# Opening stage of an int8-style cross-attention kernel: key batches ahead of the last four query tiles, query load in two parts, group 0 values quantised on GpSimd, key bias as three 16-bit parts

## The chip, the cores and the metric

One core of a Trainium2 chip. The metric is the device time of one execution in microseconds; lower is better. Names of engines: TensorE (PE, its weight loads PEld), VectorE (DVE), ScalarE (ACT), GpSimd (POOL), and SyncE (SP), whose queue issues every DMA of this kernel. Each engine works through its own instructions in the order in which they are written; semaphores tie the engines together.

## What is computed

1600 tokens of 512 channels attend with 16 heads of 32 channels to 5776 context rows, and a gated feed-forward block follows. Queries, keys, values and the softmax output are rounded to 8-bit grids:

```python
q = (x @ Wq + bq).reshape(1, B * N, H, hd)            # x: layer norm of the tokens
kv = (cond @ Wkv + bkv).reshape(1, -1, 2, H, hd)
q = _fq_sym(q * scale, axis=-1)                        # step: max|q| / 127 of a token and head
k = _fq_sym(k, axis=-1)
v = _fq_sym(v, axis=2)                                 # step over all 5776 rows
attn = _fq_unsigned(softmax(einsum('bhqd,bhkd->bhqk', q, k)), axis=-1)
out = einsum('bhqk,bhkd->bhqd', attn, v) @ Wp + bp
x = x + out;  x = x + ffn(layernorm(x))
```

## The kernel before

**Stages.** (1) The opening: the key and value projections of head group 0 (four of the sixteen heads) and the queries of all heads. (2) The loop over 200 tiles of (head, 128 tokens), i = 0 to 199, in which the projections of groups 1 to 3 are interleaved. (3) The output projection and the feed-forward block. The change is in the opening, in the first tiles of the loop, and in one matmul of every projection.

**Key units and batches.** The context is cut into 46 units of 128 rows (the last has 16). `unit(g, u)` on PE computes the keys of a unit into half of a PSUM bank (L539, four fp32 matmuls, each of which the profile shows as two), adds the key bias with a matmul of its own (L546, `e0` whose row 0 is one, times `bk_b`), and computes the values transposed (L541). Units alternate between the banks PO and PK, so a unit waits (`s_kve`) until ACT has moved out the unit two before it: `unit_out` copies keys to KB (L711) and values to VF (L713). Twelve batches of up to four units make group 0. For a batch b, DVE's `batch` takes maxima of keys and values (L877, L881) and a reciprocal (L884), POOL's `k_scale` scales KB (L1090), ACT's `k_round` rounds through int8 (L719, L724), POOL's `k_parts` (L1102, L1105, L1111) and ACT's `k_high` (L736) split the result in three bf16 parts in KS, and SP's `store_k` writes them to DRAM (L318). KS is one buffer, so parts of a batch wait (`s_kd`) for the store of the batch before it.

**Query tiles.** For each of 13 tiles of 128 tokens DVE's `layernorm(t)` takes statistics (L901 to L903), ACT takes a square root (L742, `x_sqrt`), DVE normalises (L905, L908); PE transposes (L560), ACT copies to XNT (L748), PE multiplies by WQ (L569); DVE quantises (L925 to L936) into QS, and SP stores it (L405). The order in the opening is written out by hand: PE does batch 0 and then, for t = 0 to 12, the query of tile t, the transpose of tile t + 1, and batch t + 1. DVE does layer norm t + 2, batch t, query t. ACT does the root of tile t + 2, XNT of t + 1, the four `unit_out` of batch t + 1, `k_high` of t - 1, `k_round` of t.

**The end of the opening.** SP's queue then holds, in this order: weights and first units of group 1, three quarters of head 0's keys transposed into KT (L374), the last query and key stores, the last quarter of KT, all of QT (L365), and three transposes that turn the values VI (L427). Before these DVE has quantised the values of group 0 from VF to VI (L949, L950, six instructions). Behind them stand the context loads CT (L303) of the loop's first units.

**The loop.** For tile i PE computes scores in four chunks (L592), DVE moves them out with a running minimum (L966), ACT takes exponentials to 8 bits (L790), SP transposes them (L463), POOL spreads them into PT (L1154), and four tiles later PE multiplies by the values (L611), which ACT moves to AO (L776). Between the chunks PE does quarter slices of the units of the step.

Of the kernel before, what the change touches and what calls it, by code (L numbers as in the profile page):

```python
# [39 lines left out]
P = 128  # L40
# [42 lines left out]
MAGIC = 12582912.0  # L83
LN255 = float(np.log(255.0))
EPS = 1e-5
F16_UNIT = float(2.0 ** 24)

# [45 lines left out]
def build(nc, x, ctxt, ctxl, Wq, bq, Wkv, bkv, Wp, bp, w13T, w2T, norm_w, eye, Qd, Kd, Vd, Od, out):  # L133
    ctx = ExitStack()
    with ctx:
# [8 lines left out]
        e0 = sb("e0", [P, P], F32)  # L144
        bk_b = sb("bk_b", [P, 2, GC], F32)
# [38 lines left out]
        KT = [None] * 3  # L184
        for r in (1, 0, 2):
            KT[r] = tmp(f"KT{r}", [KEYS], BF16)
        QT = ring("QT", 3, [NT * P], BF16)

        with ExitStack() as early:
            WQ = tmp("WQ", [NK, C], F32, early)  # L190
            XT = ring("XT", 2, [C], F32, early)
            XN = ring("XN", 2, [C], F32, early)
            XNT = ring("XNT", 2, [NK, P], F32, early)
            QF = tmp("QF", [H, HD], F32, early)
            QG = tmp("QG", [H, HD], F32, early)
            QS = ring("QS", 2, [H, P], BF16, early)
            BQ = tmp("BQ", [C], F32, early)
# [7 lines left out]
        AO = ring("AO", 2, [NT, 2 * HD], F32)  # L205
# [7 lines left out]
        with ExitStack() as unsplit:  # L213
# [26 lines left out]
        names = """cst s_x0 s_x1 s_w s_sd s_xn s_tp s_tpe s_q s_qe s_qs s_qd0 s_qd1 s_wg s_wg1 s_bk0 s_bk1 s_bv s_ku s_kve  # L240
                   s_kr s_kn s_ki s_kc s_k6 s_k8 s_kh s_kd s_kl s_kp s_vd0 s_vd1 s_vr s_vt s_vg s_vi s_wp s_qk s_ev s_mx s_exp s_pad s_pvp s_pv s_pve s_rz
# [55 lines left out]
        def _(sp):  # L297
# [25 lines left out]
            def load_wg(g):  # L323
                if g:
                    sp.wait_ge(M["s_ku"], g * NU)
                sp.dma_start(bk_b[:, g % 2, :], bkv[g * GC:(g + 1) * GC].partition_broadcast(P)).then_inc(M[f"s_bk{g % 2}"], 16)
                sp.dma_start(WG[:, :, 0, :], wkv_v[:, :, g * GC:(g + 1) * GC]).then_inc(M["s_wg"], 16)
                sp.dma_start(WG[:, :, 1, :], wkv_v[:, :, C + g * GC:C + (g + 1) * GC]).then_inc(M["s_wg1"], 16)
# [30 lines left out]
            def load_head(h, piece):  # L359

                if piece == 0:
# [3 lines left out]
                    sp.dma_start_transpose(QT[h % 3].rearrange("p (a n) -> p a n", a=1), Qd[:, h, :]).then_inc(s_qt[h % 3], 16)  # L365
# [10 lines left out]

            load_x(0)
            load_wg(0)
            for u in range(RING):
                load_unit(0, u)  # L380
            sp.dma_start(ident[:, :], eye).then_inc(M["s_w"], 16)
# [7 lines left out]
            for t in range(NT):  # L389
                if 2 <= t:  # L390
                    store_k(0, t - 2)
                if t + 3 < NT:
                    load_x(t + 3)
                while nxt < min(NU, NB * t + 10):
                    load_unit(0, nxt)
                    nxt += 1
                if t == NT - 1:

                    load_wg(1)
                    for u in UNITS[-1]:  # L400
                        load_unit(*u)
                    for piece in range(1, NC_):
                        load_head(0, piece)
                sp.wait_ge(M["s_qs"], t + 1)
                sp.dma_start(Qd[t * P:(t + 1) * P], QS[t % 2]).then_inc(M[f"s_qd{t % 2}"], 16)  # L405
            for b in range(NT - 2, NBT):
                store_k(0, b)
            load_head(0, NC_)

# [11 lines left out]
            sp.wait_ge(M["s_qd0"], 16 * (-(-NT // 2)))  # L421
            sp.wait_ge(M["s_qd1"], 16 * (NT // 2))
            load_head(0, 0)
            for n, lo in enumerate(VT_LO):
# [3 lines left out]
                                       VI[1][:, lo:hi, :].rearrange("p u c -> p (u c)")).then_inc(M["s_vi"], 16)  # L428
            for s in range(3):
# [92 lines left out]
        def _(pe):  # L522
            def unit(g, u, slices=range(NK)):
# [12 lines left out]
                for c in slices:  # L536
# [6 lines left out]
                    if c == 1:  # L543
                        if u == 0:
                            pe.wait_ge(M[f"s_bk{g % 2}"], 16 * (g // 2 + 1))
                        pe.matmul(bank[0:n, 0:GC], e0[:, 0:n], bk_b[:, g % 2, :], start=False, stop=True)  # L546
# [4 lines left out]
            for u in BATCH[0]:  # L551
                unit(0, u)
            pe.wait_ge(M["s_w"], 16 * 3)

# [8 lines left out]
            x_transpose(0)  # L563
            for t in range(NT):
                pe.wait_ge(M["s_tpe"], t + 1)
                if t:
# [5 lines left out]
                if t + 1 < NT:  # L572
                    x_transpose(t + 1)
                for u in (BATCH[t + 1] if t + 1 < NBT else []):
                    unit(0, u)
            for u in UNITS[-1]:
                unit(*u)

            def scores(i, c):
# [3 lines left out]
                if c == 0:  # L583
                    for h, *_r in segs:
                        pe.wait_ge(s_kt[h % 3], 16 * NC_ * (h // 3 + 1))
                        pe.wait_ge(s_qt[h % 3], 16 * (h // 3 + 1))
# [110 lines left out]
        def _(act):  # L697
# [53 lines left out]
            for u in BATCH[0]:  # L751
                unit_out(0, u)
            x_sqrt(1)
            x_transposed(0)
            for t in range(NT):
# [4 lines left out]
                for u in (BATCH[t + 1] if t + 1 < NBT else []):  # L760
                    unit_out(0, u)
# [7 lines left out]
            def values_out(i):  # L769
                p, segs = tile_of(i)  # L770
                j = i % PAIRT
                act.wait_ge(M["s_pv"], i + 1)
                if j == 0 and p >= 2:
# [76 lines left out]
        def _(v):  # L850
# [3 lines left out]
            v.memset(e0[:, :], 0.0).then_inc(chain.sem, 1)  # L854
            chain.n += 1
            chain.sync()
# [399 lines left out]
```

## Time and profile before

| | |
|---|---|
| runs shown | 2012.63, 2016.89, 2017.28 us; median 2016.89 |
| profiled execution | 2016.73 us, of it the span 2014.9 us |
| opening, until the loop's first unit has its context | 194.7 us of the span |
| PE, DVE, ACT, POOL busy over the span | 86%, 83%, 67%, 74% |
| granted PE clock, mean | 0.85 of full speed |

The profiled execution is 0.16 us from the median, so sums made against it stand for the median too. The timeline lists instructions in order of time; what stands in brackets is how long the engine was idle before it and what released it. Busy shares over the whole span mix the opening, where PE sets the pace, with the loop, where DVE does.

### The profile page before, as it was taken

How to read it: one execution, taken by the hardware profiler on the slowest of the kernel's cores; microseconds unless marked ns; L12 is line 12 of the kernel's file. 1: busy time of each engine (PE TensorE's matmuls, PEld its weight loads, DVE VectorE, ACT ScalarE, POOL GpSimd, SP SyncE). 2: the span in 40 equal slices, each digit the busy share in tenths (PEclk: the TensorE clock that was granted, in tenths of full speed). 3: DMA queues.
4: the chain of work that ended last, by engine and by line, in shares of the span. 5: the costliest groups of instructions: out<-in, count | busy, mean ns of one | idle time of the engine just before them, and what ended most of it. 6: DMA issues, size and time to landing. Idle time of an engine off the chain costs nothing.

```text
span 2014.9 us, 40535 instructions
## 1 busy us (share of the span) xinstructions
PE 1729.9 (86%) x16230; PEld 1168.7 (58%) x16230; DVE 1682.1 (83%) x2664; ACT 1357.6 (67%) x1293; POOL 1499.8 (74%) x1182
## 2 busy tenths in 40 slices
PE   7995888898788888887888888788988897699996
PEld 6884666665556666565666664344444444467774
DVE  5775999999889999997899999899999997464552
ACT  2441888888678788886888888677777776322221
POOL 1342698988898888989889889988987977255453
PEclk9997999998989999898999996566556555799998
DMA  4656899999989999999799997978877766513311
GB/s 160 204 180 176 159 199 199 185 199 189 211 173 202 178 184 187 172 213 195 166 202 193 179 194 166 186 133 166 155 140 139 149 116 116 170 43 75 77 44 43
DMA packets 862442, 323.11 MB, mean 160 GB/s; under 512 B 789104, under 2 KB 817712, under 8 KB 862256
## 3 DMA queue, kind: packets, MB, share of 16 engines
q1 hardware_dynamic: 862256, 320.53, 76.1%
q8 instruction: 129, 2.11, 0.4%
q14 instruction: 57, 0.47, 0.1%
HBM read 80.87 MB, written 46.20 MB: 63 GB/s over the span
## 4 chain that ended last, share of the span: by engine, by line
DVE 35%; PE 21%; issue 16%; POOL 15%; DMA 5%; ACT 4%; SPq 3%; POOLq 0%; DVEq 0%; ACTq 0%
DVE S L966 32%; POOL PT L1154 9%; PE PS L653 6%; PE PS L592 6%; PE PK L687 3%; DMA PP<-Pr 3%; PE PK L670 2%; PE PK L539 2%; ACT Pr L790 1%; PE PO L611 1%; SPq L463 1%; POOL VQ L1123 1%; POOL KD L1102 1%; POOL VB L1126 1%; POOL KE L1105 1%
## 5 line engine op out<-in xcount | busy, mean ns | idle before, releaser
L966 DVE TENSOR_SCALAR_CACHE_REDUCE S<-PS,SQN 128x1536 f32<-128x1536 f32 (+1 forms) x768 | 1285.7, 1714 | 90.2 <-PE PS L592 73.9
L790 ACT ACTIVATE Pr<-S,MS 128x5888 uint8<-128x5888 f32 x200 | 1041.4, 5207 | 249.7 <-DVE MJ L981 174.6
L1154 POOL CAST PT<-PP 128x1536 uint16<-128x1536 uint8 (+1 forms) x800 | 1094.5, 1413 | 93.3 <-DMA PP<-Pr 92.0
L592 PE MATMUL PS<-KT,QT 96*128 96x512 bf16 (+1 forms) x2496 | 785.7, 446 | 118.1 <-DVE S L966 106.2
L611 PEld LDWEIGHTS PO<-VI,PT 128*128 128x128 f16 x9200 | 364.6, 102 | 360.9 <-issue 185.7
L611 PE MATMUL PO<-VI,PT 128*128 128x32 bf16 x9200 | 376.4, 183 | 96.1 <-ACT AO L776 61.7
L592 PEld LDWEIGHTS PS<-KT,QT 96*128 96x128 bf16 (+1 forms) x2496 | 215.2, 108 | 316.3 <-issue 183.2
L539 PE MATMUL PK<-WG,CT 128*128 128x128 f32 (+1 forms) x1272 | 226.8, 309 | 34.0 <-DMA CT<-ctxt 20.1
L541 PE MATMUL PK<-CT,WG 128*128 128x128 f32 (+1 forms) x1272 | 210.6, 293 | 0.0
L539 PEld LDWEIGHTS PK<-WG,CT 128*128 128x128 f32 (+1 forms) x1272 | 178.0, 204 | 37.7 <-DMA CT<-ctxt 21.6
L541 PEld LDWEIGHTS PK<-CT,WG 128*128 128x128 f32 x1272 | 166.5, 193 | 1.3 <-issue 0.3
L1090 POOL TENSOR_TENSOR KB<-KB,kam 128x512 f32<-128x512 f32 (+1 forms) x48 | 48.6, 1012 | 147.4 <-DVE kam L884 147.4
L653 PE MATMUL PS<-W,XIF 128*128 128x512 f32 (+3 forms) x624 | 144.1, 387 | 3.6 <-POOL XIF L1209 3.6
L653 PEld LDWEIGHTS PS<-W,XIF 128*128 128x128 f32 (+1 forms) x624 | 114.2, 187 | 30.7 <-issue 5.4
L711 ACT ACTIVATE KB<-PK 128x128 f32<-128x128 f32 (+1 forms) x159 | 42.7, 269 | 91.8 <-PE PK L541 78.9
L1102 POOL TENSOR_TENSOR KD<-KE,kam 128x512 f32<-128x512 f32 (+1 forms) x48 | 50.6, 1055 | 70.7 <-ACT KE L724 70.7
L687 PE MATMUL PK<-W,IQF 128*128 128x512 f32 (+1 forms) x286 | 72.0, 409 | 14.5 <-POOL IQF L1203 11.5
L842 ACT ACTIVATE TG<-G 128x1408 f32<-128x1408 f32 (+1 forms) x13 | 17.9, 1377 | 79.9 <-DVE G L1043 79.9
L687 PEld LDWEIGHTS PK<-W,IQF 128*128 128x128 f32 (+1 forms) x286 | 54.5, 192 | 29.3 <-POOL IQF L1203 12.4
L1043 DVE SCALAR_TENSOR_TENSOR G<-PS,sc,TG 128x1408 f32<-128x1408 f32 (+1 forms) x13 | 21.9, 1682 | 52.3 <-PE PS L653 52.3
L546 PE MATMUL PK<-bk_b,e 128*128 128x128 f32 (+1 forms) x318 | 64.2, 285 | 0.0
L966 DVE DVE_READ_ACCUMULATOR S<-PS,SQN 128x1 f32 x768 | 63.8, 83 | 0.0
(125 smaller groups left out, 1417.5 us busy)
## 6 DMA issues: line engine op xcount, KB each, us to landing
CT<-ctxt SPq DMA_DIRECT2D x180, 256.0 KB, 3.3
k_rows<-KS SPq DMA_DIRECT2D x44, 512.0 KB, 3.9
v_rows<-VS SPq DMA_DIRECT2D x33, 256.0 KB, 3.8
VQ<-v_rows SPq DMA_DIRECT2D x33, 256.0 KB, 3.8
q_rows<-QS SPq DMA_DIRECT2D x13, 512.0 KB, 2.6
W13F<-w13T SPq DMA_DIRECT2D x16, 352.0 KB, 4.4
attn_out<-AO SPq DMA_DIRECT2D x8, 416.0 KB, 5.2
PP<-Pr SPq DMA_TRANSPOSE x200, 6.0
```

Of the source, the lines that this page charges most:

```text
L539: pe.matmul(bank[0:n, 0:GC], CT[k % RING][:, d, 0:n], WG[:, d, 0, :], start=(d == 0), stop=False)
L541: last = pe.matmul(bank[:, GC:GC + n], WG[:, d, 1, :], CT[k % RING][:, d, 0:n], start=(d == 0), stop=(d == NK - 1))
L546: pe.matmul(bank[0:n, 0:GC], e0[:, 0:n], bk_b[:, g % 2, :], start=False, stop=True)
L592: last = pe.matmul(PS[n % 2][p0:p0 + r, f:f + w], QT[h % 3][0:PARTS * HD, q0:q0 + r], KT[h % 3][0:PARTS * HD, c * CHUNK + f:c * CHUNK + f ...
L611: last = pe.matmul(PO[:, 0:w], PT[i % 2][:, u, :].bitcast(F16), VI[g % 2][:, u, h * HD:h * HD + w], start=(u == 0), stop=(u == NU - 1))
L653: last = pe.matmul(PS[half][0:n, f:f + w], XIF[:, c, 0:n], W13[:, c, a, half * FF + f:half * FF + f + w], start=(c == 0 and a == 0), stop= ...
L687: last = pe.matmul(PK[0:n, :], IQF[:, k, 0:n], W2[:, k, a, :], start=(k == 0 and a == 0), stop=(k == NF - 1 and a == WPARTS - 1))
L790: act.activation(Pr[i % 2].rearrange("p t q b -> p t b q"), S[i % 2].rearrange("p (t b q) -> p t b q", b=2, q=P), ACT.Exp, bias=MS[:, i % ...
L966: v.tensor_scalar(S[i % 2][:, c * CHUNK:c * CHUNK + CW[c]], PS[n % 2][:, 0:CW[c]], neg_step, None, ALU.mult, ALU.min, accum_out=MN[:, i % ...
L1090: gp.tensor_tensor(KA, KA, kam[:, kb % 2, 1, 0:m].unsqueeze(2).to_broadcast([P, m, HD]), ALU.mult).then_inc(M["s_kn"], 1)
L1102: gp.tensor_tensor(v3(KD), v3(KE), kam[:, kb % 2, 0, 0:m].unsqueeze(2).to_broadcast([P, m, HD]), ALU.mult).then_inc(M["s_k6"], 1)
L1154: gp.tensor_copy(PT[i % 2][:, 2 * t0:2 * t1, :].rearrange("p (t b) q -> p t b q", b=2), PP[i % 2][:, t0:t1, :].bitcast(U8).rearrange("p t ...
```

## The change

- Each of the first nine key batches (0 to 8) is followed by its query tile, as before; batches 9, 10 and 11 then follow without one, and query tiles 9 to 12 come after batch 11 (`Q_AFTER`). SP issues the transposes of KT as the batches are stored, and QT of head 0 in two parts: tiles 0 to 8 (`s_q0`) ahead of the last key stores, tiles 9 to 12 (L374 of the new file) behind the turning of the values.
- The six instructions that quantise group 0's values move from DVE to the end of POOL's opening (L1230, L1231 of the new file), behind the parts of batch 11. The scale is taken by DVE right after batch 11.
- The key bias of all groups is split by DVE, once, in three bf16 parts held in rows 0 to 2 of BK3 (seven instructions, L909 to L915); the bias matmul of every unit of every group is a bf16 one with `ones`.
- The scaling of the query by 1/sqrt(32) (L927) goes into other constants; QG is dropped.
- ACT takes the root of tile b + 2 **ahead of** `unit_out` of batch b.
- The clearing of QS comes after the start signal, that of AO moves to the start of the loop and to tile 4. DVE no longer waits for the query stores before it pads S. KT, QT and AO of the third or second buffer, and the early tiles, trade places in SBUF.

```diff
-            for t in range(NT):
-                if t + 2 < NT:
-                    x_sqrt(t + 2)
-                if t + 1 < NT:
-                    x_transposed(t + 1)
-                for u in (BATCH[t + 1] if t + 1 < NBT else []):
-                    unit_out(0, u)
-                if 1 <= t <= NBT:
-                    k_high(0, t - 1)
-                if t < NBT:
-                    k_round(0, t)
+            for b in range(NBT):
+                for t in Q_AFTER[b][:1]:
+                    if t + 2 < NT:
+                        x_sqrt(t + 2)
+                for u in BATCH[b]:
+                    unit_out(0, u)
+                if b == 0:
+                    x_transposed(0)
+                if b >= 2:
+                    k_high(0, b - 2)
+                if b:
+                    k_round(0, b - 1)
+                for t in Q_AFTER[b][:1]:
+                    x_transposed(t + 1)
...
-                        pe.matmul(bank[0:n, 0:GC], e0[:, 0:n], bk_b[:, g % 2, :], start=False, stop=True)
+                        pe.matmul(bank[0:n, 0:GC], ones[:, 0:n], BK3[:, g * GC:(g + 1) * GC], start=False, stop=True)
...
+            gp.wait_ge(M["s_vr"], 1)
+            for n, lo in enumerate(VT_LO):
+                hi = VT_LO[n + 1] if n + 1 < len(VT_LO) else NU
+                q = VF[:, lo * P:hi * P]
+                link(gp.tensor_scalar(q, q, VS3[:, 0, 2:3], MAGIC, ALU.mult, ALU.add))
+                gp.tensor_scalar(VI[1][:, lo:hi, :].rearrange("p u c -> p (u c)"), q, 1.0, -MAGIC,
+                                 ALU.mult, ALU.add).then_inc(M["s_vt"], 1)
```

ScalarE around the first units of batch 1, before (sd is the root of a tile, XNT the copy of a transpose, KB and VF the two halves of `unit_out`):

```order
L742 ACTIVATE sd<-mv 128x1 [waits s_sd]
L748 ACTIVATE XNT<-PS 128x512 [waits s_tp]
L742 ACTIVATE sd<-mv 128x1 [waits s_sd]
L748 ACTIVATE XNT<-PS 128x512 [waits s_tp]
L711 ACTIVATE KB<-PK 128x4x32 [waits s_ku]
L713 ACTIVATE VF<-PK,BV 128x128
```

The two roots are those of tiles 1 and 2; the next one, of tile 3, comes after the outputs of batch 1. ScalarE at the same place, now:

```order
L781 ACTIVATE XNT<-PS 128x512 [waits s_tp] x2
L775 ACTIVATE sd<-mv 128x1 [waits s_sd]
L744 ACTIVATE KB<-PK 128x4x32 [waits s_ku]
L746 ACTIVATE VF<-PK,BV 128x128
L744 ACTIVATE KB<-PO 128x4x32 [waits s_ku]
```

The root here is that of tile 3: it has moved one tile ahead against the outputs, and so in each of batches 1 to 8. VectorE over the same stretch, now, from the end of query 0:

```order
L984 TENSOR_SCALAR QS<-QF 128x16x96 [waits s_dve]
L950 BN_STATS st<-XT 128x6 [waits s_x1]
L951 BN_AGGR mv<-st 128x2 [waits s_dve]
L952 TENSOR_SCALAR mv<-mv 128x1 [waits s_dve]
L954 RECIPROCAL sd<-sd 128x1 [waits s_act]
```

The statistics of tile 3 stand behind the whole of query 0, as they did before. SyncE at the end of the opening, now, from the load of group 1's weights:

```order
L335 DMA WG<-Wkv 128x4x128 [waits s_ku]
L336 DMA WG<-Wkv 128x4x128
L312 DMA CT<-ctxt 128x512 [waits s_ku] x4
L427 DMA_TRANSPOSE QT<-q_rows 128x1x1152 [waits s_qd1,s_qd0]
L327 DMA k_rows<-KS 128x4x512 [waits s_kh,s_kp]
L390 DMA q_rows<-QS 128x2048 [waits s_qs]
L327 DMA k_rows<-KS 128x512 [waits s_kh,s_kp]
L330 DMA k_rows<-KS 16x512
L384 DMA_TRANSPOSE KT<-k_rows 128x1x1168 [waits s_kl,s_kd]
L390 DMA q_rows<-QS 128x2048 [waits s_qs] x3
L450 DMA_TRANSPOSE VI<-VI 128x16x128 [waits s_vt] x2
L450 DMA_TRANSPOSE VI<-VI 128x14x128 [waits s_vt]
```

Three query stores now stand ahead of the turning of the values, the last of them that of tile 12.

## Rows read from the trace of the kernel before

**Rows 1.** Windows: us, busy PE, PEld, DVE, ACT, POOL, clock, DMA share, GB/s.

```profile
160.00:180.00 20.00, 6.03 (x36) 5.84 (x36) 16.09 (x24) 2.71 (x6) 11.41 (x11) 0.66 0.80 219
```

**Rows 2.** Timeline (start, us, instruction) around the end of batch 10, PE and DVE.

```profile
142.45 1.06 PE L541 MATMUL PO<-CT,WG 128*128 128x128 f32 x8
142.84 0.69 DVE L901 BATCH_NORM_STATS2 st<-XT 128x6 f32<-128x512 f32 x1
143.34 3.60 PE L569 MATMUL PS<-WQ,XNT 128*128 128x512 f32 x8
143.78 0.15 DVE L903 TENSOR_SCALAR mv<-mv 128x1 f32<-128x1 f32 x1
146.42 0.16 DVE L905 RECIPROCAL sd<-sd 128x1 f32<-128x1 f32 x1 [2.49 <-ACT sd L742]
147.22 1.06 PE L539 MATMUL PK<-WG,CT 128*128 128x128 f32 x8
```

**Rows 3.** Timeline, the query of tile 11 on DVE, with GpSimd quiet.

```profile
155.15 0.69 DVE L925 TENSOR_TENSOR QF<-PS,BQ 128x512 f32<-128x512 f32 x1 [0.31 <-PE PS L569]
155.87 0.43 DVE L927 TENSOR_SCALAR QF<-QF 128x512 f32<-128x512 f32 x1
...
159.69 0.42 DVE L877 TENSOR_REDUCE kam<-KB 128x8 f32<-128x264 f32 x1
```

**Rows 4.** Timeline, first restart of PE in batch 0, ACT and PE.

```profile
16.65 0.20 ACT L742 ACTIVATE sd<-mv 128x1 f32<-128x1 f32 x1
17.42 1.13 PE L539 MATMUL PK<-WG,CT 128*128 128x128 f32 x8 [0.53 <-ACT VF L713]
...
20.62 1.06 PE L541 MATMUL PO<-CT,WG 128*128 128x128 f32 x8
```

**Rows 5.** Timeline, GpSimd and VectorE over each other in query 10.

```profile
152.19 1.37 POOL L1111 TENSOR_TENSOR KS<-KE 128x512 bf16<-128x512 f32 x1
...
152.69 1.15 DVE L933 TENSOR_SCALAR QG<-QG 128x512 f32<-128x512 f32 x1
```

**Rows 6.** PE after an idle stretch (timeline), and windows with the clock as in rows 1.

```profile
181.73 1.13 PE L539 MATMUL PK<-WG,CT 128*128 128x128 f32 x8 [3.10 <-ACT VS L713]
...
183.50:186.50 3.00, 3.00 (x16) 3.00 (x16) 0.00 (x0) 0.54 (x2) 0.00 (x0) 0.50 0.96 177
...
208.50:209.70 1.20, 0.00 (x0) 0.00 (x0) 1.20 (x4) 0.56 (x4) 0.00 (x0) 1.00 0.00 0
...
210.50:213.50 3.00, 3.00 (x13) 2.34 (x12) 2.87 (x7) 2.15 (x1) 0.45 (x1) 0.50 1.18 211
```

**Rows 7.** Timeline, SyncE's queue at the end of the opening, and PE's restart.

```profile
168.92 7.74 SPq L374 DMA_TRANSPOSE KT<-k_rows  x3
...
177.40 0.37 SPq L318 DMA_DIRECT2D k_rows<-KS  x1
...
181.16 1.22 SPq L374 DMA_TRANSPOSE KT<-k_rows  x1
182.48 1.57 SPq L365 DMA_TRANSPOSE QT<-q_rows  x1
184.10 7.19 SPq L427 DMA_TRANSPOSE VI<-VI  x3
191.34 2.51 SPq L303 DMA_DIRECT2D CT<-ctxt  x4
...
194.69 1.22 PE L539 MATMUL PK<-WG,CT 128*128 128x128 f32 x4 [6.43 <-DMA CT<-ctxt]
```

**Rows 8.** Groups by form on GpSimd: names, shapes, count, busy us, mean ns, idle before.

```profile
L1123 POOL TENSOR_SCALAR VQ<-VQ,VS 128x512 f32<-128x512 f32 x33 | 22.9, 693 | 20.2 <-DMA VQ<-v_rows 20.1
...
L1161 POOL TENSOR_SCALAR W<-W13F 128x2816 fp32r<-128x2816 f32 x2 | 5.1, 2542 | 0.0
```

**Rows 9.** Timeline of a unit's bias matmul and what follows it on PE.

```profile
148.11 0.39 PE L546 MATMUL PK<-bk_b,e 128*128 128x128 f32 x2
148.33 1.06 PE L541 MATMUL PK<-CT,WG 128*128 128x128 f32 x8
```

**Rows 10.** The loop from 195 to 1250: a wait (us, times, longest), a chain piece.

```profile
DVE S L966 <- PE PS L592: 61.2, 64, 7.1
...
684.88 0.28 PE PK L546 x2
```

More of the change, by code:

```diff
@@ L83 @@
 MAGIC = 12582912.0
+Q_AFTER = {b: [b] if b < 9 else [] for b in range(NBT)}
+Q_AFTER[NBT - 1] = list(range(9, NT))
+Q_HEAD = 9
 LN255 = float(np.log(255.0))
@@ L86 @@
 F16_UNIT = float(2.0 ** 24)
+QSCALE = float(1.0 / np.sqrt(np.float32(HD)))
 def plan_units():
@@ L204, in build @@
         VI.append(tmp("VI1", [NU, GC], BF16))
-        AO = ring("AO", 2, [NT, 2 * HD], F32)
+        AO = [tmp("AO0", [NT, 2 * HD], F32)]
+        with ExitStack() as early:
+            WQ = tmp("WQ", [NK, C], F32, early)
+            XT = ring("XT", 2, [C], F32, early)
+            XN = ring("XN", 2, [C], F32, early)
+            XNT = ring("XNT", 2, [NK, P], F32, early)
+            QF = tmp("QF", [H, HD], F32, early)
+            QS = ring("QS", 2, [H, P], BF16, early)
+        KT.append(tmp("KT2", [KEYS], BF16))
+        QT.append(tmp("QT2", [NT * P], BF16))
+        AO.append(tmp("AO1", [NT, 2 * HD], F32))
         stage.close()
@@ L561, in x_transpose, with query @@
                 last.then_inc(M["s_tp"], 1)
-            x_transpose(0)
-            for t in range(NT):
+            def query(t):
                 pe.wait_ge(M["s_tpe"], t + 1)
+                if t == 0:
+                    pe.wait_ge(M["s_w"], 16 * 2)
                 if t:
@@ L571, in _ @@
                 last.then_inc(M["s_q"], 1)
-                if t + 1 < NT:
-                    x_transpose(t + 1)
-                for u in (BATCH[t + 1] if t + 1 < NBT else []):
+            for b in range(NBT):
+                for u in BATCH[b]:
                     unit(0, u)
+                if b == 0:
+                    pe.wait_ge(M["s_bk"], 16 * 2)
+                    x_transpose(0)
+                for t in Q_AFTER[b]:
+                    query(t)
+                    if t + 1 < NT:
+                        x_transpose(t + 1)
             for u in UNITS[-1]:
@@ L915, in _, with query @@
             layernorm(1)
-            for t in range(NT):
+            v.wait_ge(M["s_w"], 16 * 2)
+            def query(t):
                 j = t % 2
-                if t + 2 < NT:
-                    layernorm(t + 2)
-                if t < NBT - 1:
-                    finish(batch(0, t))
+                if t:
+                    v.wait_ge(M["s_qs"], t)
                 v.wait_ge(M["s_q"], t + 1)
@@ L936, in _ @@
                 v.tensor_scalar(QS[j][:, :, 0:PARTS * HD].rearrange("p h (a d) -> p h a d", a=PARTS),
-                                QG.unsqueeze(2).to_broadcast([P, H, PARTS, HD]), -MAGIC, None,
+                                QF.unsqueeze(2).to_broadcast([P, H, PARTS, HD]), -MAGIC, None,
                                 ALU.add).then_inc(M["s_qs"], 1)
-                if t == NBT - 1:
-                    finish(batch(0, t))
+            for b in range(NBT):
+                for t in Q_AFTER[b]:
+                    if t + 2 < NT:
+                        layernorm(t + 2)
+                    if t == Q_AFTER[b][0]:
+                        finish(batch(0, b))
+                        if b == NBT - 1:
+                            v_step(0)
+                    query(t)
+                if not Q_AFTER[b]:
+                    finish(batch(0, b))
             for m in range(2):
```

155 lines of the change are left out of this document (86 added, 69 removed).

## The prediction

> **What bounds the kernel now.** I read the busy time by stretches first, then the timeline of the opening, then SyncE's queue, then the waits in the loop. The opening ends when PE gets the context of the loop's first unit, at 194.69, after 6.43 us of idleness [rows 7]. What stands ahead of that load on SyncE is a chain of its own: last key store, last piece of KT, QT, and 7.19 us of value transposes, which end at 191.3. PE did little for the 35 us before it: 6.03 us busy between 160 and 180 [rows 1]. So there is time to win there, and the loop behind it would move with it, since from there on DVE sets the pace and waits for little (61.2 us for PE in a thousand, [rows 10]). Ahead of 160 PE is the bound: between two batches stands the query, from the end of one batch (142.45 + 1.06 = 143.51) to the start of the next at 147.22, 3.71 us [rows 2], and with four units at 8.2 (twice the 4.26 of rows 4, less the drain between pairs) a period is 11.91 us. There DVE waits for ACT's root (2.49 us, [rows 2]); PE waits for nobody.
>
> **What the moved root does.** This is the step on which the forecast rests. Before, the outputs of batch b stand on ACT behind the root of tile b + 1, whose statistics DVE took before query b - 1. Now they stand behind the root of tile b + 2, whose statistics stand on DVE behind the whole of query b - 1. And PE's third unit of batch b waits for the output of the first. So a loop closes through PE, DVE and ACT in each of batches 1 to 8. Its length, from the end of batch b - 1: PE's query product begins 0.17 us earlier (143.34 against 143.51) and takes 3.60 us, and DVE starts 0.04 us later: 3.47. DVE's query took 155.15 to 159.69, 4.54 us, with GpSimd quiet; without the scaling (0.43 and its gap, to 0.47) that is 4.07 [rows 3]. Statistics: 142.84 to 143.93, 1.09 [rows 2]. The root starts 0.04 us later; from its start to PE's restart 16.65 to 17.42, 0.77; then two units, 17.42 to 21.68, 4.26, less twice the bias saving of 0.16 (below), 3.94 [rows 4]. The sum is 13.38 us. Without the loop the period would be 11.91 - 4 x 0.16 = 11.27. So PE stands still for some 2.1 us in each of eight periods, and two surcharges come on top.
>
> The first is GpSimd. Its parts of batch b - 1 run while DVE is in query b: the 0.43 us addition of L933 took 1.15 us when L1111 ran, and ended 0.28 us behind it [rows 5]. It costs at most 1.3 us for a query (the two instructions so stretched in query 10), at least nothing; a moved phase leaves perhaps one of them: 0.5.
>
> The second is PE's clock. After 3.10 us of idleness PE ran at full clock for a while, then at half from 183.5 to 186.5, though it was busy; after a wait of 1.2 us at 208.5 came the same, 210.5 to 213.5 at 0.50, that is at 1.2 instead of 2.4 GHz [rows 6]. A stretch of 3 us or a little more at half clock loses about 1.5 us of work, and here it would fall on the last two units and the next query product, which are all on the loop. Bounds 0 and 3.4; I take 1.5, by these two rows. The period becomes 13.38 + 0.5 + 1.5 = 15.4, eight of them 123.2 us. The Trainium skill, TensorE: Matmul & The Clock Gate, section "HAM oscillation", lets a TensorE that waits between bursts fall back to the lower clock, but only for longer waits than these. By that rule the term of 1.5 is nothing, and the sum is the first rival's; these rows speak against it.
>
> **The start.** PE can begin earlier, since the clearing of AO and QS (some 4.4 us of DVE) no longer precedes it, but its first bias matmul waits until DVE has cut the bias in parts: seven instructions of 0.43 to 0.72 us, about 4.3 us from some 7.7, to 12.0 against 11.5 now. ACT then has the roots of tiles 0, 1 and 2 ahead of the first output, and the third needs a token load that follows the first normalisation. Layer norm 0 and 1 end at about 15.5 and 17.7, the load lands at about 19.5, statistics and root make it 20.7, and PE's third unit starts at 21.3 instead of 17.42. Batch 0 ends at about 25.2 instead of 21.68; bounds 24 and 28.
>
> **To the end of batch 10.** Batch 8 ends at 25.2 + 123.2 = 148.4. Batch 9 takes the query's 3.71 and four units, about 7.6, 11.3 in all; batch 10 takes 7.4, and 1.0 for a context load that stands behind a transpose of KT on SyncE (each 1.2 to 3.5 us; bounds 0 and 3). That is 168.1. Before, batch 11 was done at 151.6.
>
> **The tail**, counted from the end of batch 10. Batch 11 ends at 3.9, the product of query 9 at 7.4, DVE's query 9 at 12.7 (with 1.2 us of GpSimd), layer norm 12 and its root take it to 14.9, query 10 to 19.1; query 11 begins at 19.4. GpSimd cannot start the values sooner: its last key part waits for the store of batch 10, which on SyncE stands behind a transpose of KT (7.74 for three, [rows 7]), weights, context and the first part of QT, and goes out at 14.3. A store took 177.40 to 181.16 to land with its small companion; with 3.6 us and the part's 0.6 the values start at 18.5. They are six instructions of about 1.9 us: from L1161, 2542 x 2048 / 2816 = 1.85; from L1123, at most 4 x 0.693 = 2.8 [rows 8]. Three instructions of each DVE query (product, addition, QS) want what GpSimd holds. Each then waits for the end of one of these, up to 1.9 us, where before it was 1.4 at most. I walked the two engines against each other: query 11 ends at 27.6 and query 12 at 33.1, against 23.5 and 28.4 without that. The Trainium skill, SBUF — State Buffer, section "Who interferes with whom", has the same: one exclusive lock for DVE's and GpSimd's shared ports. A split bandwidth instead would leave the tail some 4 us shorter; rows 5 speak for the lock. The rest is SyncE: store 0.45, the turning of values 7.2, the second part of QT 0.5, the context load 3.35 until PE goes on (191.34 to 194.69) [rows 7]. Restart at 44.7, or 40.0 without GpSimd's hold. The early part of QT buys nothing: scores could start, but PE's second slice still waits for that context. So the restart is at 168.1 + 44.7 = 212.8 instead of 194.69: 18.1 us later. DVE's quantising of the values, 8.4 us of the old tail, is gone from DVE, but query 12 now stands where it stood.
>
> **In the loop.** AO's clearing costs DVE 0.75 us at tile 4. The bias matmul: it takes 0.22 us (148.11 to 148.33, [rows 9]); in bf16 I put it at 0.06, by a score matmul of four times the columns, three of which took 0.66. 138 units times 0.16 are 22 us of PE, but PE is not the bound: the chain passes a bias matmul about once in 30 us of the K-producing loop, as at 684.88 [rows 10], 19 pieces of 5.4 us together. Three quarters of that, 4 us; bounds 0 and 22.
>
> **The sum.** 2016.7 + 18.1 + 0.75 - 4.0 = 2031.6 us. Other removals (waits for query stores, L927's time in the tail) are in the steps above; the changed places in SBUF cost nothing, as nothing waits for them.
>
> **The rivals.** First, the clock stays up in the short waits: 8 x 1.5 = 12 less, 2019.6. Second, the loop through the root does not close, because DVE is done with the query and the statistics before ACT needs the root. Then batches 1 to 8 stay at 11.27 us, eight times 4.1 less, and the time is 1998.6: faster. It decides at 3.9 us, from the product's end to the point (7.4 after the batch) at which PE's third unit wants its bank; DVE needs 5.2 at least by rows 2 and 3, which is why it gets little. Third, PE sets the pace of the loop after all, so that all 22 us of bias matmuls count: 2013.6. For it speaks that DVE's waits end on PE; against it that they sum to 61 us, part of them at phase changes where GpSimd and the transposes are late.
>
> **How the numbers follow.** Forecast 0.66, its own range 2021 to 2046 by the bounds of start, contention, clock and tail; clock rival 0.12; root rival 0.12; pace rival 0.10. A difference of 0.3%, 6 us, is about what a measurement can tell from no change. Faster: the root rival and some of the pace rival, 0.16; within 0.3%: 0.17; slower: 0.67. The range leaves out the root rival and the far end: 2010 to 2046.
>
> **What would show it.** In the profile after: ACT's root in batches 1 to 8 released by DVE's statistics, and PE idle about 2 to 3 us before each third unit, in periods of 15.4 us (step wrong if 11.3); half clock in some of each period; batch 11 done at about 172 instead of 152; DVE's L980, L981, L984 stretched to 2 us while GpSimd has the values; the first unit of the loop at about 213. It would be wrong if PE showed no wait for ACT there, or if the loop from its first unit to the feed-forward part took more than 5 us less than before.

## The result and the profile after

The changed kernel takes 2035.91 us (median of four runs, 2033.92 to 2037.70) against 2017.09 for the kernel before (four runs on the same chip, 2012.63 to 2018.04). The ratio is 1.0097, with a 95% interval from 1.0078 to 1.0117: slower by 1.0%. (Below, such an interval stands in brackets behind a ratio.) The profiled execution took 2037.41 us with a span of 2035.6, 20.7 above the span of before. The page's line of busy time and its chain:

```profile
PE 1721.5 (85%) x16046; PEld 1146.6 (56%) x16046; DVE 1671.8 (82%) x2651; ACT 1356.0 (67%) x1293; POOL 1505.4 (74%) x1188
...
DVE 40%; PE 26%; issue 12%; POOL 11%; DMA 5%; ACT 4%; SPq 1%; DVEq 0%; POOLq 0%; ACTq 0%
```

Over the whole span the busy shares are within a point or two of those of before, so they do not say where 20 us went. The stretches do.

Waits of the changed kernel between 25 and 165 us (engine, line and what it waited for: us in total, times, longest):

```profile
ACT sd L775 <- DVE mv L952: 40.1, 8, 5.1
ACT KB L744 <- PE PK L567: 24.4, 11, 3.5
PEld PK L565 <- issue: 22.3, 8, 2.9
PE PK L565 <- ACT VF L746: 21.0, 8, 2.7
```

The first row is ACT's root waiting for DVE's statistics, once in each of batches 1 to 8; the last is PE standing still ahead of each third unit, 1.86 us in batch 1 and 2.73 in the seven others. Neither stood there before: in [rows 2] DVE waited for the root, and PE for nobody. One turn of the loop, in batch 3: DVE's statistics end, ACT takes the root and then the first output, and PE goes on.

```profile
67.16 0.15 DVE L952 TENSOR_SCALAR mv<-mv 128x1 f32<-128x1 f32 x1
67.35 0.20 ACT L775 ACTIVATE sd<-mv 128x1 f32<-128x1 f32 x1 [5.12 <-DVE mv L952]
...
67.61 0.36 ACT L746 ACTIVATE VF<-PK,BV 128x128 f32<-128x128 f32 x1
...
68.12 1.13 PE L565 MATMUL PK<-WG,CT 128*128 128x128 f32 x8 [2.73 <-ACT VF L746]
```

Two periods in the timeline of PE (start, us, instruction, idle time before it and its releaser):

```profile
37.65 1.33 PE L565 MATMUL PK<-WG,CT 128*128 128x128 f32 x8 [1.86 <-ACT VF L746]
...
38.88 2.02 PE L567 MATMUL PK<-CT,WG 128*128 128x128 f32 x8
...
43.14 3.60 PE L592 MATMUL PS<-WQ,XNT 128*128 128x512 f32 x8
...
53.70 1.13 PE L565 MATMUL PK<-WG,CT 128*128 128x128 f32 x8 [2.73 <-ACT VF L746]
...
54.72 1.11 PE L567 MATMUL PK<-CT,WG 128*128 128x128 f32 x8
```

The matmuls of one unit took 2.02 us in one period and 1.11 in the next. The windows round the first of them (us, busy PE, PEld, DVE, ACT, POOL, clock, DMA share, GB/s) show why: PE was busy throughout, at 1.2 instead of 2.4 GHz, right behind the wait of 1.86 us.

```profile
35.00:38.40 3.40, 1.54 (x15) 1.38 (x14) 2.48 (x6) 1.05 (x5) 0.00 (x0) 1.00 0.52 148
38.40:41.50 3.10, 3.10 (x17) 3.04 (x16) 0.00 (x0) 0.54 (x2) 0.00 (x0) 0.51 0.00 0
41.50:50.00 8.50, 8.50 (x54) 6.50 (x53) 4.54 (x9) 2.28 (x5) 4.15 (x4) 0.98 0.46 155
```

The tail, DVE's query 11 first. [rows 3] gave 4.54 us for a whole query, with GpSimd quiet. Here the same query took far longer:

```profile
190.77 0.69 DVE L974 TENSOR_TENSOR QF<-PS,BQ 128x512 f32<-128x512 f32 x1 [2.05 <-PE PS L592]
191.50 0.69 DVE L976 TENSOR_REDUCE am<-QF 128x16 f32<-128x512 f32 x1
192.22 1.10 DVE L977 TENSOR_SCALAR am<-am 128x16 f32<-128x16 f32 x1
193.35 1.92 DVE L978 TENSOR_SCALAR SQN<-am 128x16 f32<-128x16 f32 x1
195.18 0.24 DVE L979 RECIPROCAL am<-am 128x16 f32<-128x16 f32 x1
195.45 2.31 DVE L980 TENSOR_TENSOR QF<-QF,am 128x512 f32<-128x512 f32 x1
197.80 1.87 DVE L981 TENSOR_SCALAR QF<-QF 128x512 f32<-128x512 f32 x1
199.70 2.32 DVE L984 TENSOR_SCALAR QS<-QF 128x1536 bf16<-128x1536 f32 x1
202.05 0.69 DVE L974 TENSOR_TENSOR QF<-PS,BQ 128x512 f32<-128x512 f32 x1
```

GpSimd in the same stretch, the last key part and then the values:

```profile
188.72 0.61 POOL L1166 TENSOR_TENSOR KS<-KE 128x256 bf16<-128x256 f32 x1 [5.62 <-DMA k_rows<-KS]
189.32 1.99 POOL L1230 TENSOR_SCALAR VF<-VF,VS 128x2048 f32<-128x2048 f32 x1
191.39 1.90 POOL L1231 TENSOR_SCALAR VI<-VF 128x2048 bf16<-128x2048 f32 x1
193.27 1.98 POOL L1230 TENSOR_SCALAR VF<-VF,VS 128x2048 f32<-128x2048 f32 x1
195.33 1.90 POOL L1231 TENSOR_SCALAR VI<-VF 128x2048 bf16<-128x2048 f32 x1
197.20 2.19 POOL L1230 TENSOR_SCALAR VF<-VF,VS 128x1792 f32<-128x1792 f32 x1
199.47 1.74 POOL L1231 TENSOR_SCALAR VI<-VF 128x1792 bf16<-128x1792 f32 x1
```

Lay the two over each other: L978, which writes 16 columns and takes 0.17 us elsewhere, ends at 195.27, when the GpSimd instruction begun at 193.27 ends; L980 runs over 197.2 and L981 over 199.4, where GpSimd's next two ends lie. Query 11 takes 11.25 us. SyncE's queue and PE's restart, which answer to [rows 7]:

```profile
183.20 0.53 SPq L327 DMA_DIRECT2D k_rows<-KS  x1
...
206.85 7.47 SPq L450 DMA_TRANSPOSE VI<-VI  x3
214.42 1.73 SPq L374 DMA_TRANSPOSE QT<-q_rows  x1
216.19 2.00 SPq L312 DMA_DIRECT2D CT<-ctxt  x4
...
219.19 1.12 PE L565 MATMUL PK<-WG,CT 128*128 128x128 f32 x4 [4.46 <-DMA CT<-ctxt]
```

The restart is at 219.19 instead of 194.69, 24.5 us later, and the span is 20.7 longer. In this pair of profiles the difference of 3.8 came back in the loop. There a bias product now holds up the next matmul for 0.06 us, where [rows 9] showed 0.22 (the first number is the start, the second the length; the next matmul starts while the product's end is still under way):

```profile
153.75 0.22 PE L572 MATMUL PK<-BK,ones 128*128 128x128 bf16 x1
153.81 1.11 PE L567 MATMUL PK<-CT,WG 128*128 128x128 f32 x8
```

### The profile page after: what moved, and what is told of

Its sections match the earlier page's. It is cut to its first block, busy times and chain, and to the rows that moved or that the text cites. A ratio compares the mean times of both kernels' runs of the same rounds, so it can differ in the third digit from the quotient of the medians.

```text
span 2035.6 us, 40165 instructions
## 1 busy us (share of the span) xinstructions
PE 1721.5 (85%) x16046; PEld 1146.6 (56%) x16046; DVE 1671.8 (82%) x2651; ACT 1356.0 (67%) x1293; POOL 1505.4 (74%) x1188
## 4 chain that ended last, share of the span: by engine, by line
DVE 40%; PE 26%; issue 12%; POOL 11%; DMA 5%; ACT 4%; SPq 1%; DVEq 0%; POOLq 0%; ACTq 0%
DVE S L1017 33%; PE PS L625 7%; POOL PT L1209 7%; PE PS L686 6%; DMA PP<-Pr 3%; PE PK L720 3%; PE PK L565 3%; PE PS L592 2%; ACT Pr L834 2%; PE PK L703 2%; PE PO L644 1%; PE PK L567 1%; POOL VQ L1178 1%; POOL VB L1181 1%; DVE kam L927 1%
## 5 line engine op out<-in xcount | busy, mean ns | idle before, releaser
L565 PE MATMUL PK<-WG,CT 128*128 128x128 f32 (+1 forms) x1272 | 227.6, 310 | 43.9 <-ACT VF L746 23.5
L567 PE MATMUL PK<-CT,WG 128*128 128x128 f32 (+1 forms) x1272 | 217.4, 300 | 0.0
L565 PEld LDWEIGHTS PK<-WG,CT 128*128 128x128 f32 (+1 forms) x1272 | 178.5, 205 | 48.6 <-issue 42.6
L567 PEld LDWEIGHTS PK<-CT,WG 128*128 128x128 f32 x1272 | 171.1, 198 | 1.7 <-issue 0.3
L720 PE MATMUL PK<-W,IQF 128*128 128x512 f32 (+1 forms) x286 | 71.7, 408 | 15.2 <-POOL IQF L1265 11.6
L927 DVE TENSOR_REDUCE kam<-KB 128x16 f32<-128x528 f32 (+1 forms) x48 | 32.4, 676 | 52.3 <-ACT VF L746 52.3
```

What stands on the lines that cost most here:

```text
L565: pe.matmul(bank[0:n, 0:GC], CT[k % RING][:, d, 0:n], WG[:, d, 0, :], start=(d == 0), stop=False)
L567: last = pe.matmul(bank[:, GC:GC + n], WG[:, d, 1, :], CT[k % RING][:, d, 0:n], start=(d == 0), stop=(d == NK - 1))
L720: last = pe.matmul(PK[0:n, :], IQF[:, k, 0:n], W2[:, k, a, :], start=(k == 0 and a == 0), stop=(k == NF - 1 and a == WPARTS - 1))
L927: chain.mark(v.tensor_reduce(K_[:, 0, 0:n * GH], KB[kb % 2][:, 0:n].rearrange("p n h d -> p (n h) d"), X, ALU.max, apply_absolute_value=True))
```

## Experiments

"Restart" below is the start of the first four matmuls (L565) of the first unit in the loop. Ratios are to the kernel before, run beside each on the same chip.

**The root's place.** On ACT, in root_back:

```diff
-                for t in Q_AFTER[b][:1]:
-                    if t + 2 < NT:
-                        x_sqrt(t + 2)
                 for u in BATCH[b]:
                     unit_out(0, u)
...
                     k_round(0, b - 1)
                 for t in Q_AFTER[b][:1]:
+                    if t + 2 < NT:
+                        x_sqrt(t + 2)
                     x_transposed(t + 1)
```

> The changed kernel with one thing undone: the root of tile b + 2 stands again behind the outputs of batch b on ACT, not ahead of them. My theory (the loop of PE's third unit, ACT's root and DVE's statistics sets the period of batches 1 to 8, and the clock falls because of the wait in it): PE no longer waits for ACT's output ahead of each third unit (21.0 us in eight waits now), the period from one query product to the next falls from 15.3 to about 11.3 us, 8 x 4.0 = 32 us less, and some 2 us more at the start, where the third root no longer precedes the first outputs. The first unit of the loop at 219.2 - 34 = 185, time about 2002, ratio to before 0.993. Rival A (the changed kernel's batches are long for another reason, such as GpSimd's lock or the shifted key rounding): waits move elsewhere, period 14 or more, time above 2025. Rival B (the opening's gain is given back in the loop): restart at 185, but time above 2015.

Measured: 2000.98 us, ratio 0.9935 [0.9911, 0.9959], restart 187.44. The query products start 11.45 to 11.55 us apart (eight times, from 23.61 to 115.35). Among the waits between 22 and 120 us DVE is again the one that waits for the root, and there is none of PE ahead of a third unit:

```profile
DVE sd L953 <- ACT sd L775: 24.4, 9, 4.6
```

The expected numbers came to within 2.5 us. One line on ACT is worth 31.7 us of the restart, and with it back the rest of the change makes the kernel faster than before. Both rivals fell.

**The clock.** In filler, on PE:

```diff
                 for u in BATCH[b]:
+                    if 1 <= b <= 8 and u == BATCH[b][2]:
+                        for _ in range(10):
+                            pe.matmul(PS[0][:, 1024:1024 + P], ident[:, :], ident[:, :], start=True, stop=True)
                     unit(0, u)
```

> The changed kernel plus ten products of the identity with itself (128 columns, 32-bit, into a bank that nobody reads there) on PE ahead of the third unit of batches 1 to 8, so that PE is busy for about 2.1 of the 2.7 us in which it waits there now. Outputs are untouched. My theory (the half clock in every second period comes from that wait): the clock stays up, all eight periods take about 14.4 us instead of 14.42 and 16.05 in turn, so about 4 x 1.6 = 6.5 us less, restart at about 213, time about 2029. Rival (the 16.05 us periods have another cause, such as GpSimd's stretching of DVE or the parity of buffers): periods alternate as before, time within 2 us of 2035.9; and if the filler delays the third unit, up to 8 x 2 us more.

Measured: ratio 1.0091 [1.0066, 1.0116], restart 213.88. From the second product on, at 41.91, six periods in a row are 14.41 to 14.43 us and the seventh is 14.58, and the clock no longer falls:

```profile
36.00:50.00 14.00, 14.00 (x105) 11.99 (x104) 7.44 (x17) 3.87 (x12) 4.15 (x4) 1.00 0.43 140
50.00:64.00 14.00, 13.51 (x99) 11.33 (x98) 7.61 (x16) 4.90 (x14) 4.16 (x4) 1.00 0.50 163
```

In the changed kernel 14.42 and 16.05 alternate. With the wait filled no period is long, so the waits brought the half clock, though only every second one of them did. Why only those stays open. The restart moved by 5.3 us, where 6.2 were expected. That is 0.0026 of the time, less than the intervals of the two ratios can tell, so the time shows neither that it followed nor that it did not.

**Who holds DVE.** In v_act the six instructions on values run on ACT, in v_dve on DVE behind the last query, as before. The edit in v_act, on ACT behind the transposed tile 12 (L1230 and L1231 leave GpSimd; MG holds the constant of the rounding and its negative):

```diff
+                act.activation(q, q, ACT.Identity, bias=MG[:, 0:1], scale=VS3[:, 0, 2:3]).then_inc(M["s_va"], 1)
+                act.wait_ge(M["s_va"], n + 1)
+                act.activation(VI[1][:, lo:hi, :].rearrange("p u c -> p (u c)"), q, ACT.Identity,
+                               bias=MG[:, 1:2]).then_inc(M["s_vt"], 1)
```

> The changed kernel with the values of group 0 quantised on ACT (six instructions, behind the transposed tile 12) instead of on GpSimd. My theory (GpSimd's values hold the shared port, so that DVE's query 11 takes 11.25 us and query 12 4.4): without them query 11 on DVE takes 4.1 to 4.5 us, the last query ends at about 199.5 instead of 206.4, the first unit of the loop starts at about 212 instead of 219.2, time about 2029, ratio 1.006. Rival (query 11 is long for another reason, or ACT's quantising comes late and takes the place of GpSimd's): query 11 still above 8 us, or the turning of the values waits for ACT; restart at 217 or later, time within 2 us of 2035.9.

> The changed kernel with one part undone: the values of group 0 are quantised on DVE behind the last query, as before the change, not on GpSimd. My theory (GpSimd's instructions on values hold the port that DVE's 16-bit outputs, multiplications and additions need, and so lengthen queries 10 to 12): query 11 on DVE takes 4.1 us instead of 11.25 and the last query ends near 198.5 instead of 206.4; DVE then works 8.4 us on the values, but the turning runs beside it piece by piece, and PE goes on at about 214.5 instead of 219.2: 4.5 us less than the changed kernel, ratio to before about 1.0075. Rival (moving the values off DVE was worth its 8.4 us): restart at 219 or later, ratio 1.0097 or more.

v_act: ratio 1.0060 [1.0039, 1.0082], restart 210.85. v_dve: 1.0062 [1.0042, 1.0082], restart 214.68. Query 11 on DVE takes 4.2 us in both. In v_act, the instructions that took 1.92 and 2.31 us above:

```profile
190.73 0.17 DVE L990 TENSOR_SCALAR SQN<-am 128x16 f32<-128x16 f32 x1
...
191.09 0.69 DVE L992 TENSOR_TENSOR QF<-QF,am 128x512 f32<-128x512 f32 x1
```

and DVE's own first instruction on values, in v_dve:

```profile
199.75 1.29 DVE L1006 TENSOR_SCALAR VF<-VF,VS 128x2048 f32<-128x2048 f32 x1
```

So GpSimd's work on the values was the cause, and the rivals of both expectations fell. To take the values off DVE, 7.2 us of work in v_dve (199.75 to 206.95), made the restart 4.5 us later, not earlier. DVE needs 1.29 us where GpSimd needs 1.99, and in v_dve the turning (the three transposes of VI) starts at 202.33, beside the second piece, where in the changed kernel it starts at 206.85, behind the last query.

**The bias product in the loop.** no_bias is the kernel before with the product left out in groups 1 and up (their keys get no bias); bias_more is the changed kernel with a 32-bit product with zeros added there.

```diff
-                    if c == 1:
+                    if c == 1 and g == 0:
                         if u == 0:
```

```diff
+                        if g:
+                            pe.matmul(bank[0:n, 0:GC], Z[:, 0:n], WG[:, 0, 0, :], start=False, stop=False)
                         pe.matmul(bank[0:n, 0:GC], ones[:, 0:n], BK3[:, g * GC:(g + 1) * GC], start=False, stop=True)
```

> The kernel before, without the bias product in groups 1 and up (the keys of these groups get no bias; group 0 and the opening are as before). PE has 0.22 us less in each of about 138 units of the loop, 30 us. My theory (DVE sets the pace, PE's bias products are on the path for a fifth to a quarter of their time): the opening unchanged, the restart at about 194.7, the loop 5 to 8 us shorter, ratio to before about 0.997. Rival 1 (PE sets the pace): 30 us less, ratio 0.985. Rival 2 (what the changed kernel won back in the loop is only the spread between runs): ratio 1.000.

> The changed kernel plus one 32-bit product of 128 columns with a zero operand, ahead of the bias product of every unit in the loop (groups 1 and up, not in the opening). It costs PE what the old bias product cost, about 0.22 us for each of 115 units or so, 25 us in all, and adds zero to the keys. My theory (DVE sets the pace of the loop, PE's bias products are on the path for about a quarter of their time, and the 16-bit bias product won about 4 us there): 4 to 8 us more, about 2042. Rival 1 (PE sets the pace): about 25 us more, 2060. Rival 2 (the loop's 3.8 us came from something else, the bias product is hidden): within 1.5 us of 2035.9.

no_bias: ratio 0.9968 [0.9953, 0.9982], 6.4 us less for 138 x 0.22 = 30 us taken from PE. bias_more: 1.0134 [1.0114, 1.0154] against 1.0097, 7.5 us more for 30 added (its expectation counted 115 units; there are 138). Both give a fifth to a quarter, with wide intervals: 3.6 to 9.5 us in the first, and some 2 to 13 in the difference of the second. So PE does not set the pace, and a bias product is not free either.

**The query load.** one_qt loads head 0's queries in one part, at the second part's place (the edit's main lines):

```diff
-            sp.dma_start_transpose(QT[0][:, 0:Q_HEAD * P].rearrange("p (a n) -> p a n", a=1),
-                                   Qd[0:Q_HEAD * P, 0, :]).then_inc(M["s_q0"], 16)
```

> The changed kernel with the query load of head 0 in one part again, at its last place, so that the early transpose of nine tiles does not stand on SyncE ahead of the store of key batch 10. My theory (the early part buys nothing, since PE waits for the context behind the turning anyway): the first scores go no later than PE's second slice needs, the last key stores go 1.6 us earlier, and with them the values on GpSimd and the restart: 217 to 219 instead of 219.2, ratio to before 1.008 to 1.0097. Rival (the early part lets the scores start sooner and is worth 2 us or more): restart above 221, ratio above 1.0105.

Measured: 1.0092 [1.0059, 1.0125], no difference to 1.0097 that can be told. The restart was 221.10, 1.9 us later and not earlier: my theory was wrong here, and the rival's sign for the restart came true, though not its ratio. The store of key batch 10 went out at 181.83 instead of 183.20, but the last key store stayed where it was (189.71 against 189.41). GpSimd gained nothing (its values started at 189.67 against 189.32), and the first scores now waited for QT:

```profile
219.13 1.44 PE L618 MATMUL PS<-KT,QT 96*128 96x512 bf16 x3 [4.54 <-DMA QT<-q_rows]
```

So in these profiles the early part saves a wait of the first scores, 1.9 us of the restart, and costs nothing that shows further on.

**Queries between batches, and a better tail.** q_late2 is root_back with `Q_AFTER = {b: [b]}` for all batches but the last, which has queries 11 and 12, and `Q_HEAD = 11`. tail1 is root_back with the two edits below (the three lines of the loads leave their old place behind the turning). best3 and best4 put q_late2's queries and tail1's edits together, best3 with values on ACT, best4 with the store of key batch 10 ahead of the first part of the query load.

```diff
+            for s in range(3):
+                for g, u in UNITS[s]:
+                    load_unit(g, u)
             for n, lo in enumerate(VT_LO):
                 sp.wait_ge(M["s_vt"], n + 1)
...
-            act.wait_ge(M["s_pad"], 2)
...
+                if i == 0:
+                    act.wait_ge(M["s_pad"], 2)
```

> The kernel with the root moved back (root_back), with one more part undone: a query after every batch and only queries 11 and 12 after the last, as before the change, instead of batches 9, 10 and 11 in a row and queries 9 to 12 after them; the first part of the query load then covers 11 tiles. My theory (in the tail queries run one by one, about 6.5 us each, since product, quantising and bank wait for each other, while between batches a query costs 3.7): the product of query 11 near 146.5, the last query on DVE ends near 160 instead of 174.5, GpSimd's values end near 172, and PE goes on near 180 instead of 187.4: 7 us less than root_back, ratio to before about 0.990. Rival (the key batches in a row bring the last key store and KT early, and that sets the end): restart at 187 or later, ratio 0.9935 or more.

> root_back with another order in the tail: SyncE issues the context loads of the loop's first units ahead of the turning of the values and the second part of the query load, and ACT waits for the padding of S only ahead of its first exponential, not ahead of the outputs of group 1. My theory (the restart hangs on SyncE's queue, 7.5 us of turning, 1.8 of the query part and the load behind them, and on the 16 us wait of ACT for the padding, none of which the first scores need): scores start as soon as DVE is done with query 12, DVE's second score slice at about 179 instead of 188.95, the time 8 to 10 us below root_back, ratio to before about 0.989. Rival (DVE is only shifted and the loop waits later for the values of tile 0): gain under 3 us, ratio 0.992 or more, with a new wait of PE for the turned values.

> All that the runs point to: root moved back, a query after every batch, values of group 0 quantised on ACT (two pieces ahead of the last rounded keys, one behind), context loads ahead of the turning, ACT's wait for the padding ahead of the first exponential. If each works as I think, the last query on DVE ends near 160, scores start near 163 to 168, 20 us before those of root_back, time about 0.983 of before. Rival (ACT's 12 us on values delay the last keys and so KT): scores near 175, ratio 0.988.

> The tail of tail1 (context loads ahead of the turning, ACT's wait for the padding ahead of the first exponential) with q_late2's queries between the batches, values on GpSimd as in the changed kernel, and the store of key batch 10 ahead of the first part of the query load. My theory: in q_late2 the last key store waited behind that load and for its landing (key stores at 157.85 and 165.26, last piece of KT at 167.2), then 9 us of turning; now the last KT piece goes out near 162 and scores start near 165 instead of 175.9 (tail1), while GpSimd's values run behind the last query and hold nobody on the path. Time about 8 us below tail1, ratio to before about 0.982. Rival (the values for tile 0 or the last key batch come late and the loop gives it back): ratio 0.986, as tail1.

| kernel | ratio, 95% | restart | restart to the fourth output store |
|---|---|---|---|
| before | 1 | 194.69 | 877.2 |
| no_bias | 0.9968 [0.9953, 0.9982] | 194.62 | 868.3 |
| changed | 1.0097 [1.0078, 1.0117] | 219.19 | 874.1 |
| bias_more | 1.0134 [1.0114, 1.0154] | 217.53 | 878.1 |
| filler | 1.0091 [1.0066, 1.0116] | 213.88 | 874.7 |
| v_act | 1.0060 [1.0039, 1.0082] | 210.85 | 868.5 |
| v_dve | 1.0062 [1.0042, 1.0082] | 214.68 | 872.9 |
| one_qt | 1.0092 [1.0059, 1.0125] | 221.10 | 865.8 |
| root_back | 0.9935 [0.9911, 0.9959] | 187.44 | 866.4 |
| q_late2 | 0.9876 [0.9849, 0.9904] | 182.77 | 867.1 |
| tail1 | 0.9857 [0.9833, 0.9882] | 177.99 | 864.9 |
| best3 | 0.9869 [0.9848, 0.9890] | 175.80 | 867.4 |
| best4 | 0.9856 [0.9831, 0.9881] | 173.17 | 875.9 |

tail1 did what was expected: scores start on DVE right behind its last query, and its second slice at 179.38 (expected near 179). The time fell by more than the 8 to 10 us expected, from 0.9935 to 0.9857; the intervals leave 9 to 23 us.

```profile
175.09 0.75 DVE L1004 MEMSET AO<- 128x832 f32 x1
175.87 1.82 DVE L1016 TENSOR_SCALAR_CACHE_REDUCE S<-PS,SQN 128x1536 f32<-128x1536 f32 x1
```

q_late2 was expected to restart near 180 and did at 182.77; GpSimd's last key part stood until 164.57 behind a store, and the values and their turning behind it. best3 and best4 started their scores on DVE at 175.77 and 171.01, not at 163 to 168 and 165. In best4 PE was on the first units of group 1 until 169.84, and the last piece of KT, which went out at 166.49, let its scores go at 170.15. In best3 it was ACT: it worked on the values until 168.96, PE's third unit of group 1 waited for it until 169.53, and the scores behind it started at 174.92. That is what best3's rival said (near 175), though not by way of KT. best4's rival came true in the ratio: 0.9856, as tail1. Its restart is 4.8 us earlier than tail1's, but that is 0.0024 of the time, and the two intervals cannot tell it from nothing. Both are 1.4% faster than the kernel before.

The last column is what the profiles say of the loop. Behind the restart the work is nearly the same in all these kernels but before, no_bias and bias_more (in tail1, best3 and best4 the order at the loop's start differs), and yet it takes 865 to 876 us to the fourth store. The stores of outputs, of tail1 and then of best4 (third and fourth in each):

```profile
842.73 0.44 SPq L439 DMA_DIRECT2D attn_out<-AO  x1
...
1042.91 0.51 SPq L439 DMA_DIRECT2D attn_out<-AO  x1
```

```profile
842.82 0.43 SPq L439 DMA_DIRECT2D attn_out<-AO  x1
...
1049.06 0.51 SPq L439 DMA_DIRECT2D attn_out<-AO  x1
```

They are level at the third store, though best4 restarted 4.8 us earlier, and 6 us apart at the fourth. Over that stretch DVE was busy alike (182.28 and 182.31 us), waited for PE 15.2 and 19.6 us, and the granted clock was 0.94 and 0.92. But these are single executions. The profiled one of tail1 was the fastest of its four (1984.41 us, median 1989.65), that of best4 the slowest (1993.55, median 1988.50), and the kernel before, with nothing changed, ran from 2008.74 to 2022.15 us in 17 executions. So differences of up to 11 us in the last column need no other cause than that spread. Whether the moment of entry changes how the engines meet in the loop, as I had supposed, is not shown. What makes the spread stays open, and so does how much of the 3.8 us won back in the changed kernel is the bias product's. A fifth of its 22 us, by no_bias, gives 4.6, which would fit, but one pair of profiles can't show it.

## The prediction, step by step

The forecast was 2031.6 us, slower, and that is what came. The sum missed by 4.3 us, mostly by the tail.

- **The loop through the root: right.** Predicted period 15.4, measured 15.3 on average ((149.16 - 26.74) / 8), with ACT waiting for statistics and PE standing still eight times, once for 1.86 and seven times for 2.73 us; predicted 2.1. Without it 11.46 against 11.27 predicted. root_back shows the cause. The rival "the loop does not close" priced the other case at 1998.6; root_back, where it is open, has 0.9935 x 2017.09 = 2004.
- **The clock: the mechanism was right, its course not.** I put 1.5 us on every period. It was 1.6 on every second one and none on the others: at half clock behind the wait of 1.86 us and three of those of 2.73, at full clock behind the other four of 2.73. At full clock the loop takes 14.42, where I had 13.38 + 0.5 = 13.88, and the clock adds 0.8 on average, where I had 1.5. These two misses nearly cancel, so that the period came out right is in part luck. Of the 0.54 us by which the loop is longer, 0.35 is GpSimd's hold, which I had at 0.5: a query of DVE takes 4.92 us to the next statistics (61.30 to 66.22, with L977 and L980 lengthened by 0.28 and 0.57), where query 0, with GpSimd quiet, took 4.08 (31.67 to 35.75). That a short wait of PE can bring the half clock was read from [rows 6]; filler, at a clock of 1.00 from 28 to 160 us, shows it for these waits. The Trainium skill's rule, in TensorE: Matmul & The Clock Gate, section "HAM oscillation", which asks for longer waits, did not hold here, with half clock behind 1.86 and 2.73 us: the measurement decides.
- **The start:** batch 0 ended at 26.74 instead of 25.2, inside the bounds. The third unit started as predicted (21.08 against 21.3), behind the third root; the bias parts were ready at 13.2 instead of 12.0, and the third unit ran mostly at half clock behind a wait of 2.53 us (21.08 to 24.58, its value product 2.02 us instead of 1.11), which I had not put in. This step and the two batches behind the loop leave the end of batch 10 at 169.26 against 168.1.
- **The tail: mis-sized, 49.9 us against 44.7.** Query 11 began at 21.5 instead of 19.4, as its product ran mostly at half clock (5.27 us instead of 3.60) behind a wait of 3.42 us for DVE: the effect that I had priced in the loop and forgot here. Query 11 took 11.25 us instead of 8.2. I had let three instructions of a query wait for GpSimd; five did, L977 and L978 with 16 columns among them, since each began while a GpSimd instruction ran. Query 12 took 1.1 less than I had. SyncE took 12.7 instead of 11.5, since the second part of QT took 1.73 instead of 0.5. That it is a hold (a DVE instruction stands until GpSimd's has ended) and not shared bandwidth was right: L978, 16 columns and 0.17 us by itself, took 1.92 us and ended with GpSimd's instruction, and v_act shows that GpSimd was the holder. The Trainium skill, SBUF — State Buffer, section "Who interferes with whom", has that lock; the trace agrees.
- **GpSimd's values:** they started 20.1 us after batch 10 instead of 18.5, because the store of key batch 10 took 5.5 us to land, not 3.6 (issued at 183.20, GpSimd went on at 188.72).
- **The loop:** predicted 3.25 us won (4.0 less 0.75), 3.8 in the profiles, a difference that single executions cannot confirm. no_bias, scaled to 22 us, gives 4.6 for the bias and bias_more 5.5, where I had 4.0. The pace rival, all 22 us, is out.
- **The query load in two parts:** I had said that the early part buys nothing. The restart of one_qt is 1.9 us later without it, because the first scores then wait for QT and PE's next slice stands behind them. In the time that is too little to be seen.

The range of 2010 to 2046 held the time. The restart alone was 6.4 us later than predicted (219.19 against 212.8), and 0.55 more than predicted came back in the loop: that is the 5.8 us by which the profiled execution lies above the forecast.

## What to carry to other kernels

When an operation moves on an in-order engine, follow what it waits for: a root of 0.2 us, put ahead of the outputs of a batch, tied PE to the end of a whole DVE phase and cost 32 us of the restart, over eight periods and the start. Count a short wait of PE up to twice, once as idleness and once as the half clock that may follow it, and look for every wait of the kind, not only the one at hand: here the second price fell due behind half of them, and once more in the tail. And before work goes to GpSimd, ask what DVE does meanwhile: the values were slower there (1.99 against 1.29 us an instruction) and stretched a query from 4.2 to 11.25 us. Last, a gain of under 5 us in an opening can be read from the restart but not from four runs of 2000 us each.

## What the hardware showed beyond this

Of seven waits of equal length (2.73 us) three were followed by half clock and four were not; the first, of 1.86 us, was. Periods with half clock and full clock took turns, and with the waits filled (filler) all ran at full clock. A DVE instruction over 16 columns, 0.17 us by itself, took 1.92 us beside GpSimd's instructions of 1.9 us: its small size did not protect it. And the same rounding of 128x2048 values took 1.29 us on DVE, 1.99 on GpSimd and 2.08 on ACT.
